# The output stage's gather: slots no longer cleared, dropped picks read a row of zeros

## The reference, cut to what matters

```
order = jnp.argsort(-priority)
pos = jnp.take_along_axis(jnp.cumsum(oneh, axis=0) - 1, tiF[:, None], axis=1)[:, 0]
keep = pos < cap
slot = jnp.where(keep, tiF * cap + pos, E * cap)
buf = jnp.zeros((E * cap + 1, C), xf.dtype).at[slot].set(xrep)
h = gelu(einsum('ecd,edf->ecf', buf[:-1].reshape(E, cap, C), W1) + b1)
y = jnp.einsum('ecf,efd->ecd', h, W2) + b2[:, None, :]
yf = jnp.concatenate([y.reshape(E * cap, C), jnp.zeros((1, C), y.dtype)], axis=0)
gate = jnp.where(keep, wo.reshape(-1), 0.0)
contrib = yf[slot] * gate[:, None]
```

## Time and profile before

| | |
|---|---|
| runs | 6634.27 to 6637.27 us, median 6634.87 |
| profiled execution, its own time | 6633.88 us |
| its span, first to last instruction | 6632.1 us |
| mean granted TensorE clock | 0.863 of full |
| PE busy | 4831.6 us (73%) |
| POOL busy | 3834.9 us (58%) |
| DVE busy | 2371.6 us (36%) |
| ACT busy | 1459.2 us (22%) |
| output phase's first and last gather issue | 4038.5 and 6484.0 us |

### The profile page before, as it was taken

The page is one execution under the profiler, slowest core; times in us unless marked ns, Lnnn a source line. Parts: engine busy times, 40 slices in busy tenths (PEclk is TensorE's granted clock), DMA queues, the critical chain, the costliest instruction groups (busy, mean ns, idle before and its releaser), DMA issues. The chain is left out here.

```text
span 6632.1 us, 69063 instructions
## 1 busy us (share of the span) xinstructions
PE 4831.6 (73%) x20564; PEld 2709.5 (41%) x20564; DVE 2371.6 (36%) x4527; ACT 1459.2 (22%) x3608; POOL 3834.9 (58%) x3737
## 2 busy tenths in 40 slices
PE   9999996102777979877987783466776677777778
PEld 4555666101444444434544441233333333333334
DVE  0012248970222222212222222444445545444442
ACT  2233344500222323222332230000000010000001
POOL 0000000008887888778877825777777777777770
PEclk9999998555888989888998896688888888888889
DMA  8877779812333333232333223222222222222210
GB/s 170 185 185 196 192 201 275 286 56 65 100 98 103 108 97 89 86 86 85 101 89 87 74 58 106 81 87 91 89 88 76 70 72 71 93 76 76 76 39 29
DMA packets 840381, 711.46 MB, mean 107 GB/s; under 512 B 596030, under 2 KB 681668, under 8 KB 836048
## 3 DMA queue, kind: packets, MB, share of 16 engines
q1 hardware_dynamic: 666320, 466.30, 25.8%
q0 software_dynamic: 109312, 139.69, 7.8%
q10 hardware_dynamic: 64512, 102.79, 4.5%
HBM read 440.11 MB, written 385.75 MB: 125 GB/s over the span
## 5 line engine op out<-in xcount | busy, mean ns | idle before, releaser
L1077 POOL DMA_INDIRECT y_ring<-ye,index_o x1568 | 1675.3, 1068 | 539.9 <-issue 452.1
L758 POOL DMA_INDIRECT xe<-chunk,index x1568 | 1539.6, 982 | 477.4 <-issue 476.1
L1110 PE MATMUL cp<-padded,taps_o 128*128 128x448 f32 x4032 | 1623.5, 561 | 49.8 <-DVE padded L1296 49.8
L1110 PEld LDWEIGHTS cp<-padded,taps_o 128*128 128x128 f32 x4032 | 785.5, 198 | 816.2 <-issue 795.6
L887 ACT ACTIVATE hid<-hid_ps,b_cols 128x448 f32<-128x448 f32 x1120 | 709.4, 633 | 1663.2 <-PE hid_ps L841 1565.1
L849 PE MATMUL y_ps<-hid,w_sb 128*128 128x448 f32 x2240 | 918.5, 554 | 0.4 <-DVE yt L912 0.4
L841 PE MATMUL hid_ps<-xt,w_sb 128*128 128x448 f32 x2240 | 890.9, 541 | 1.5 <-DVE xt L906 1.5
L1241 DVE SCALAR_TENSOR_TENSOR z<-y_ring,gates,z 128x128 f32<-128x128 f32 x1568 | 432.0, 347 | 905.0 <-DMA y_ring<-ye,index_o 890.1
L470 POOL MEMSET zeros<- 98x512 f32 x1 | 0.5, 524 | 1109.7 <-POOLq L105 1109.7
L1174 ACT ACTIVATE outb<-cp,shift,s 128x448 f32<-128x448 f32 x224 | 162.1, 723 | 2175.0 <-PE cp L1110 2175.0
L906 DVE COPY xt<-xt_ps 128x448 f32<-128x448 f32 x280 | 174.9, 625 | 1280.8 <-PE xt_ps L832 1278.2
(11 more groups left out here) (190 smaller groups left out, 3862.1 us busy)
## 6 DMA issues: line engine op xcount, KB each, us to landing
xe<-zeros SPq DMA_DIRECT2D x16, 3920.0 KB
rows_in<-xe SPq DMA_DIRECT2D x280, 224.0 KB, 2.6
ye<-rows_out SPq DMA_DIRECT2D x280, 224.0 KB, 2.3
xin<-in_x_dram SPq DMA_DIRECT2D x256, 196.0 KB
conv<-rows ACTq DMA_DIRECT2D x256, 196.0 KB
pix<-conv SPq DMA_DIRECT2D x224, 224.0 KB, 5.1
xn<-hat SPq DMA_DIRECT2D x112, 448.0 KB, 4.4
chunk<-xn POOLq DMA_DIRECT2D x112, 448.0 KB, 3.9
```

The costliest lines, as they stand in the source:

```text
L758: pool.indirect_dma_start(out=xe[:, :], out_offset=bass.IndirectOffsetOnAxis(ap=index[ch][:, c, j:j + 1], axis=0), in_=chunk[ch][:, j * C: ...
L1077: pool.indirect_dma_start(out=y[ch][c][:, j * C:(j + 1) * C], out_offset=None, in_=ye[:, :], in_offset=bass.IndirectOffsetOnAxis(ap=index[ ...
L1110: last = pe.matmul(cp[i % 2][:, 0:HB * W], taps[:, t, :], padded[b][:, img, hb * HB + kh:hb * HB + kh + HB, kw:kw + W], start=(t == 0), st ...
```

## The change

A row of zeros is added behind the last slot of `ye`; SP writes it in the route phase, behind the zeros of `xe`. The gather's limit is raised by one, so that a dropped pick reads that row. The memset of the gather buffer, its semaphore and the wait for it go. The scatter into `xe` keeps its limit.

```
-            sp.wait_ge(zeroed, 16 * ZD)
+            sp.dma_start(ye[DROP:DROP + 1, :], zeros[0:1, 0:C]).then_inc(zeroed, 16)
+            sp.wait_ge(zeroed, 16 * (ZD + 1))
...
-        cleared = sem("cleared")
...
                     set_index(n + 1, (ch + 1) % NCHK)
                     if first and ch == NCHK - 1:
                         pool.wait_ge(const_turned, 10)
-                    pool.memset(y_ring[:, ch * 2 * CC:(ch + 1) * 2 * CC], 0.0).then_inc(cleared, 1)
-                    pool.wait_ge(cleared, n + 1)
                     for j in range(CHK):
                         for c in range(2):
                             pool.indirect_dma_start(
                                 out=y[ch][c][:, j * C:(j + 1) * C], out_offset=None, in_=ye[:, :],
                                 in_offset=bass.IndirectOffsetOnAxis(ap=index[ch][:, c, j:j + 1], axis=0),
-                                bounds_check=s["DROP"] - 1, oob_is_err=False).then_inc(y_in[ch], 16)
+                                bounds_check=s["DROP"], oob_is_err=False).then_inc(y_in[ch], 16)
...
-    ye = nc.dram_tensor("ye", (s["DROP"], C), F32).ap()
+    ye = nc.dram_tensor("ye", (s["DROP"] + 1, C), F32).ap()
```

More of the change, by code:

```diff
@@ L394, in _, with route_phase @@
                 chunk(m)
-def route_phase(nc, s, logits, xe, slots, gates, needed):
+def route_phase(nc, s, logits, xe, ye, slots, gates, needed):
     PR, J, CAP, DROP, TILES = s["PR"], s["J"], s["CAP"], s["DROP"], s["TILES"]
@@ L1314, in build @@
             conv_norm_phase(nc, s, x, dw_kernel, dw_bias, bands, conv, xn, ln_gamma, ln_beta, Wg, bg, logits)
-            route_phase(nc, s, logits, xe, slots, gates, needed)
+            route_phase(nc, s, logits, xe, ye, slots, gates, needed)
         expert_phase(nc, s, xn, xe, ye, slots, needed, ln_beta, W1, b1, W2, b2, layer_scale)
```

## The result

The changed kernel takes 6468.42 us (median of 4 runs, 6459.45 to 6489.38) beside 6634.57 us of the kernel before: ratio 0.9754, 95% interval 0.9729 to 0.9778. I forecast 6424 us, from 6378 to 6458. The sign was right; 44 us of the forecast gain were missing, and the time lies outside the range.

A forecast was written before the change was run, and what follows sets the result against it. The prediction took POOL's gather issue to bound the output phase. The shorter seam's 226 us less 15 given back made 211 us; from the profiled 6633.88 that gives 6422.9, and 1.0 for the median made 6424 us, range 6378 to 6458.

The forecast's parts named there:

- The bound: Output phase: the end follows POOL's gather issue, so each microsecond POOL saves before its last gather should move the end.
- The seam: POOL between two chunks' gathers: 3.57 us falls to 1.55, saving 2.02 us in each of 112 chunks, 226 us.
- What is given back: POOL's gather DMAs held under DVE's weight multiplications: 1 us lost in each of 15 pairs, 15 us; bounds 0 and 40.
- the rival in which nothing is held: POOL's gather DMAs beside DVE's multiplications: DVE does not hold them at all, a faster outcome; chance 0.03.
- What is added on the queues: Gather queue: dropped picks now move bytes, 0.25 us per engine in every 1.31, hidden by POOL's spacing; costs 0 to 1 us.
- The rival of the slow row: Late gathers reading one row at 36 GB/s are slow; at 23 GB/s 460 us more, about 7095 us; chance 0.05.
- The range: Whole kernel: 6378 to 6458 us, taking in the long seam bound in part and the short seam as a whole.
- the sum: Whole kernel: 226 us from the seam less 15 given back, 211 us saved, predicting 6424 us.
- What is late next: Output phase's PE and DVE loop: at least 121 us a pair against POOL's 139, so POOL stays the bound by 18.
- The row's store: Route phase, SP's queue: one more DMA, hidden with 150 us to spare; uncovered it would cost under 4 us.

The follow-up runs named there:

- once-only: Kernel before with its memset in the first pair alone and no row of zeros: 6409.6 us (0.9655); on the other kind of chip 7345.23 us (1.0858).
- f4: Changed kernel, still one row of zeros, with four output buffers between ACT and its stores in place of two: 6459.77 us (0.973 to the kernel before).
- h2: Changed kernel with memset and wait kept, the one row of zeros still read: 6641.71 us (1.0011 to the kernel before).
- h1: Changed kernel with two neighbouring rows of zeros, half of the partitions reading each: 6400.84 us (0.9647 to the kernel before).
- f3: Changed kernel with 128 rows of zeros, one for each partition, in place of one: 6400.69 us (0.9642 to the kernel before).
- f1: The changed kernel again, no edit, on another chip: 6550.71 us (0.9869 to the kernel before).
- e3: Kernel before with its memset in the first pair alone, no row of zeros, on the other kind of chip: 7345.23 us (1.0858).

## Why the prediction was wrong

*The bound* was right for POOL's part: POOL's issue ended 238 us earlier, and 2.16 us a chunk came out of the seam. It did not hold for the end: in the late pairs the chain runs through the output's stores. *The seam* was taken at 1.55 us and measured 1.41: behind an index write the gather is issued 0.16 us after the write ends, not 0.30. That is 112 x 2.16 = 242 us in place of 226.

*What is given back* came out at 1568 x (1097 - 1068) ns = 45 us more on the DMAs and 113 x (534 - 250) ns = 32 less on the index writes, 13 us against 15 forecast. Part of that agreement is luck. The 15 are the difference of two estimates for one pair, 9.0 and 8.0 us, while my count over the phase had 9 us a pair before as well, which would give back nothing; and the DMAs' mean rose by 29 ns, not by 17, and the writes' stayed at 250, not 223. That DMAs are held under DVE's tensor_tensor is confirmed by the higher mean and by the changed kernel's timeline: from 4918.21 us on four gathers in a row took 3.02, 3.16, 3.03 and 3.15 us, and each ended 0.87 to 0.88 us after one of DVE's four instructions (4920.36, 4923.82, 4927.15 and 4930.62 us). So the rival in which nothing is held, at 0.03, did not come. What it is in a gather DMA that is held is not shown.

*What is added on the queues* is the step that failed: I put it at 0 to 1 us, and it cost 64 us behind POOL. I drew a line through two stretches of the kernel before, in which every read goes to a row of its own, and got 0.25 us of an engine for a full gather, hidden in 1.31. That number is right for full gathers (0.24 us with 128 rows), but not for reads that meet in one row: 1.08 us, with gathers, z loads and stores all behind it. I then costed late landings by the gather alone, of which only the last is on the path. The first to be hurt was the queue of another engine, the output's stores, because ACT has only two buffers.

*The rival of the slow row* had the cause but not the way. It let DVE's sums and POOL wait for landed buffers; measured, DVE's sums waited less for gathers than before, 500.8 us against 890.1, POOL waited 0.3 us, and the stores' landing stopped ACT and PE. Its demand of 36 GB/s took the undisturbed pace of 18.6 us a chunk; with the held time it is 33 GB/s (426 gathers in 600 us), and the row served 32 to 34. So demand and supply lay next to each other, and a part of the gain had to go. I priced the rival at 23 GB/s only, as a reversal, and let the range in which it eats a part of the gain fall out of the forecast. Its evidence, the 46 GB/s of gamma_r's load, is what the queue reached here for all its rows, while the one row had 32 to 34 of it; a chance of 0.05 was too small beside a demand that I had put at 36.

*The range* fell short for this reason: 44 us from the forecast, 10 us above its upper end. Without the one row the sum holds on the low side: 6634.6 - 211 = 6424 forecast, 6400.69 and 6400.84 measured with the rows spread, 16 of the 23 us between being the seam's.

*What is late next* was right for idle queues: the once-only version shows no wait of POOL for DVE at 138 us a pair; how much is to spare was not measured. *The row's store* cost nothing that shows: the expert phase's first DMA is issued at 1469.61 us, before at 1471.72.

*Why the stores land so late* is only in part shown. From 5600 to 6200 us the changed kernel's queue 0 takes 76.7% of the engines' time, queue 1, the loads by its 25.69 MB, 13.7% and queue 10, the output stores by its 13.04 MB, 5.7%, 96% together; before it was 5.1, 13.2 and 5.6%, 24% together. With four output buffers (f4) the stores landed 2.6 us after issue in the median from 4200 to 4800 us, and 29.1 us from 5600 to 6200 us, where the shares add up to 100%. So they are late where the engines are full, and the gathers' packets fill them. How an engine shares its time between the queues, and with it how many us of the 15 to 33 come from the gathers' 1.08 us, no run shows.

## What to carry to other kernels

Masked or padded gather indices that all point at one dummy row can make that row the limit (here at 32 to 34 GB/s): give each partition a row of its own, or split the reads over at least two rows, or keep finite leftovers in the buffer and let a zero gate take them out. When a kernel's gather gets faster, compute the demand on its hottest address, not only the bytes, and look which other queue has the fewest buffers behind the same DMA engines. A pause that looks like waste on POOL, between bursts of indirect DMAs, may be what keeps the other engines going on some chips (without it, once-only, 3.5% faster on one kind and 8.6% slower on the other): time its removal on more than one. And where a rival's threshold lies beside the demand, price the near miss too, not only the collapse.

## What the runs showed of the hardware

One 512-byte row of DRAM served 32 GB/s of reads beside other queues' work and 34 GB/s without (f4); at 30 GB/s the queue kept up, landings at 5.4 us (h2). Two neighbouring rows took 33 GB/s together and the gathers landed in 2.8 us in the median (h1). A gather of 128 full rows takes 0.24 us of each DMA engine when the rows differ (f3); when 92 of them are one, 0.88 at one gather in 1.57 us (h2) and 1.08 to 1.12 at one in 1.41 to 1.47 (the changed kernel, f1, f4). On one of two kinds of chip PE issued its matmuls 1.4 to 2.8 us apart, in place of 0.38, in two stretches that began 26 and 29 us after POOL had started a run of gathers (e3); the cause is open.
